# Transposed attention scores of two heads as row tiles, with one exponential over two banks, in a fused attention and mixture-of-experts block

## The reference

```python
Q, K, V = (x @ qw), (x @ kw), (x @ vw)          # 16 heads of 8
Q, K = rope(Q, freq), rope(K, freq)
score = einsum('bhqd,bhkd->bhqk', Q, K) / sqrt(8)
score = score - 1e10 * (1 - causal)
score = score - max(score, axis=-1)
attn = einsum('bhqk,bhkd->bhqd', softmax(score), V)
x = layernorm(x + merged @ ow)
gates = top-2 of softmax(x @ router_w + router_b), renormalised
h = silu(x @ w1[e]) * (x @ w3[e]);  out = sum_e gates[e] * (h @ w2[e])
x = layernorm(x + out)
```

## Time and profile before

| | |
|---|---|
| time, median of 3 runs | 498.72 us (497.11 to 499.74) |
| span of the profiled execution | 495.2 us |
| mean granted TensorE clock | 0.962 |
| projections, rope and pass S of group 0 | 0 to 58 us |
| seven `STEADY` stages | 58 to about 299 us |
| `LAST` | about 299 to 331 us |
| expert phase | 331 to 495 us |

### The profile page before, as it was taken

How to read it: one execution, slowest core, us unless ns; L and a number is a source line. 1 busy time by engine, 2 the same in 40 slices (tenths; PEclk the granted TensorE clock), 3 DMA queues, 4 the chain that set the end, 5 groups by cost and what they waited for, 6 DMA issues and landing times.

```text
span 495.2 us, 10480 instructions
## 1 busy us (share of the span) xinstructions
PE 463.4 (94%) x2676; PEld 296.0 (60%) x2676; DVE 323.8 (65%) x802; ACT 285.1 (58%) x594; POOL 166.9 (34%) x167
## 2 busy tenths in 40 slices
PE   5779999999999999999999999989999999999992
PEld 2346555555554654655655545447887787787781
DVE  3879757777677676777776774313656756756743
ACT  1311146765766766767657666956565565565560
POOL 4524010230411402402304112126645564564661
PEclk9986579999999999999999999999999999999997
DMA  7877411212112112202121000000000000000000
GB/s 249 267 226 192 122 21 26 68 33 66 40 19 64 40 19 64 57 18 67 37 65 39 3 1 3 2 0 1 1 1 3 21 0 0 21 0 0 22 0 22
DMA packets 41738, 23.49 MB, mean 47 GB/s; under 512 B 31280, under 2 KB 33968, under 8 KB 41712
## 3 DMA queue, kind: packets, MB, share of 16 engines
q1 hardware_dynamic: 41712, 23.18, 17.1%
HBM read 14.26 MB, written 8.65 MB: 46 GB/s over the span
## 4 chain that ended last, share of the span: by engine, by line
PE 77%; DVE 7%; issue 4%; ACT 4%; DMA 4%; SPq 3%; POOL 1%; DVEq 0%; ACTq 0%; POOLq 0%
PE bank L960 20%; PE bank L975 15%; PE bank L1044 14%; PE bank L938 14%; PE bank L1055 7%; DVE maxima L703 2%; PE bank L993 2%; DMA k_scratch<-rope_lo 2%; PE bank L941 2%; ACT num L600 1%; DVE num L763 1%; DVE num L836 1%; ACT num L539 1%; SPq L314 1%; PE bank L1020 1%
## 5 line engine op out<-in xcount | busy, mean ns | idle before, releaser
L539 ACT ACTIVATE num<-bank 128x512 f32<-128x512 f32 (+3 forms) x384 | 168.8, 495 | 101.6 <-PE bank L960 99.1
L703 DVE TENSOR_REDUCE maxima<-bank 128x1 f32<-128x512 f32 (+15 forms) x384 | 182.3, 519 | 66.9 <-PE bank L941 46.2
L960 PE MATMUL bank<-q_op,k_op 128*128 128x512 f32 (+3 forms) x384 | 148.2, 419 | 2.8 <-ACT num L539 1.7
L938 PE MATMUL bank<-k_op,q_op 128*128 128x512 f32 (+15 forms) x384 | 126.3, 369 | 3.4 <-issue 2.9
L437 POOL TENSOR_SCALAR_AFFINE_SELECT num<-num 128x512 f32<-128x512 f32 x64 | 40.6, 635 | 226.0 <-ACT num L539 224.1
L960 PEld LDWEIGHTS bank<-q_op,k_op 128*128 128x128 f32 x384 | 71.4, 197 | 69.1 <-ACT num L539 62.0
L468 POOL TENSOR_TENSOR q_op<-num,q_op 128x512 fp32r<-128x512 f32 x64 | 82.4, 1290 | 63.6 <-ACT q_op L593 60.3
L938 PEld LDWEIGHTS bank<-k_op,q_op 128*128 128x128 f32 x384 | 77.0, 202 | 19.2 <-DVE maxima L703 10.9
L1044 PE MATMUL bank<-q_op,w_hi 128*128 (+1 forms) x256 | 81.9, 401 | 1.7 <-DVE num L836 1.6
L975 PE MATMUL bank<-num,v_op 128*32 128x512 f32 (+3 forms) x768 | 82.5, 503 | 0.0
L836 DVE TENSOR_TENSOR num<-bank,num 128x512 f32<-128x512 f32 x64 | 44.2, 691 | 58.5 <-ACT num L600 54.8
(11 more groups left out here) (86 smaller groups left out, 315.7 us busy)
## 6 DMA issues: line engine op xcount, KB each, us to landing
k_op<-k_scratch SPq DMA_DIRECT2D x16, 256.0 KB, 2.7
q_op<-q_scratch SPq DMA_DIRECT2D x64, 52.0 KB
w_raw<-in_w_all SPq DMA_DIRECT2D x6, 512.0 KB, 4.3
q_scratch<-rope_hi SPq DMA_DIRECT2D x8, 256.0 KB, 3.1
k_scratch<-rope_hi SPq DMA_DIRECT2D x8, 256.0 KB, 3.6
xT<-in_x_feat SPq DMA_DIRECT2D x4, 256.0 KB, 6.1
k_scratch<-k_op SPq DMA_DIRECT2D x2, 512.0 KB, 6.2
q_scratch<-rope_lo SPq DMA_DIRECT2D x4, 256.0 KB, 3.9
```

What stands on the lines that cost most here:

```text
L539: act.activation(num[:, t % PB, h, off:CH], t_bank[k % TB][:, off:CH], ACT.Exp, scale=scale)\
L703: dve.tensor_reduce(maxima[:, half, j:j + 1], s_bank[k % SB][:, 0:width], AX.X, ALU.max)\
L938: ins = pe.matmul(s_bank[k % SB][:, 0:width], q_op[u][:, j, :, :].rearrange("p h q -> p (h q)"), k_op[u][:, lo:lo + width], start=True, st ...
L960: pe.matmul(t_bank[k % TB][:, off:CH].rearrange("p (j q) -> p j q", q=QD), k_op[w][:, kt * P:(kt + 1) * P], q_op[w][:, c * NB + off // QD: ...
```

## The change

Pass T now takes two heads in one step. Each of the two matmuls uses only its own head's 32 partitions of `k_op` and `q_op`, as a row tile of the array at row 32 x head, and they write into two neighbouring banks; one ScalarE instruction then takes the exponential over both banks (2 x up to 512 values on each partition). The T steps of a stage become 24. The T side has two pairs of banks, four in all, and the S side keeps two banks. The places of `MROWS`, `NORM` and the `C` steps are renumbered to the new count of T steps, and the interleaving list comes out of the same rule with the new counts.

```diff
+HP = GH // 2
-T_UNITS = [(c, kt, h) for c in range(NC) for kt in range(TI * (c + 1)) for h in range(GH)]
+T_UNITS = [(c, kt, h) for c in range(NC) for kt in range(TI * (c + 1)) for h in range(HP)]
-SB = 3
-TB = 3
+SB = 2
+TB = 2
-C_FROM, C_EVERY = 4, 3
+C_AT = [2 + 3 * r // 2 for r in range(C_STEPS)]
-MROWS_AT, NORM_AT, MROWS0_AT, NORM0_AT = 5, 12, 19, 25
+MROWS_AT, NORM_AT, MROWS0_AT, NORM0_AT = 2, 6, 9, 12
...
-        bank = [ctx.enter_context(nc.psum_tensor(f"bank{i}", [P, CH], F32)) for i in range(8)]
-        s_bank, t_bank, o_bank, small_bank = bank[0:3], bank[3:6], bank[6], bank[7]
+        s_bank = [ctx.enter_context(nc.psum_tensor(f"s_bank{i}", [P, CH], F32)) for i in range(SB)]
+        t_bank = [ctx.enter_context(nc.psum_tensor(f"t_bank{i}", [P, 2, CH], F32)) for i in range(TB)]
...
-                        act.activation(num[:, t % PB, h, off:CH], t_bank[k % TB][:, off:CH], ACT.Exp, scale=scale)\
+                        act.activation(num[:, t % PB, 2 * h:2 * h + 2, off:CH], t_bank[k % TB][:, :, off:CH], ACT.Exp, scale=scale)\
                             .then_inc(t_exped, 1)
...
-                        pe.matmul(t_bank[k % TB][:, off:CH].rearrange("p (j q) -> p j q", q=QD),
-                                  k_op[w][:, kt * P:(kt + 1) * P],
-                                  q_op[w][:, c * NB + off // QD:(c + 1) * NB, h, :], start=True, stop=True)\
-                            .then_inc(t_ready, 1)
+                        for i in range(2):
+                            head = 2 * h + i
+                            rows = slice(head * QD, (head + 1) * QD)
+                            ins = pe.matmul(t_bank[k % TB][:, i, off:CH].rearrange("p (j q) -> p j q", q=QD),
+                                            k_op[w][rows, kt * P:(kt + 1) * P],
+                                            q_op[w][rows, c * NB + off // QD:(c + 1) * NB, head, :],
+                                            start=True, stop=True, tile_position=(head * QD, 0))
+                        ins.then_inc(t_ready, 1)
```

More of the change, by code:

```diff
@@ L45 @@
 SEG_T = [sum(u[0] == c for u in T_UNITS) for c in range(NC)]
-NPV = NT // GH
-SB = 3
-TB = 3
+NPV = NT // HP
+SB = 2
+TB = 2
 HB = 4
@@ L60 @@
 S_LATE, S_EARLY = 0, 3
-MROWS_AT, NORM_AT, MROWS0_AT, NORM0_AT = 5, 12, 19, 25
+MROWS_AT, NORM_AT, MROWS0_AT, NORM0_AT = 2, 6, 9, 12
 def stage_plan(with_s, with_t):
     s_units = S_UNITS if with_s else []
-    t_units = [(u, 0) for u in T_UNITS[GH:]] if with_t else []
-    t_units += [(u, 1) for u in T_UNITS[:GH]] if with_s else []
+    t_units = [(u, 0) for u in T_UNITS[HP:]] if with_t else []
+    t_units += [(u, 1) for u in T_UNITS[:HP]] if with_s else []
     def s_work(units):
@@ L94, in stage_plan @@
         plan.append(("T", c, kt, h, ahead))
-        if not with_s and at >= C_FROM and (at - C_FROM) % C_EVERY == 0 and (at - C_FROM) // C_EVERY < C_STEPS:
-            plan.append(("C", (at - C_FROM) // C_EVERY))
+        if not with_s and at in C_AT:
+            plan.append(("C", C_AT.index(at)))
         part = min(1, t_work(t_units[S_LATE:x + 1]) / max(1, t_work(t_units[S_LATE:len(t_units) - S_EARLY])))
@@ L100, in stage_plan @@
             done_s += 1
-        if h == GH - 1 and with_t and not with_s:
-            t = at // GH - 2
+        if h == HP - 1 and with_t and not with_s:
+            t = at // HP - 2
             if t >= 0:
@@ L107, in stage_plan @@
                 plan.append(("OCOPY", 0))
-        elif h == GH - 1 and with_t:
+        elif h == HP - 1 and with_t:
             if kt >= 1:
@@ L168, in sem @@
             return ctx.enter_context(nc.semaphore(name))
-        bank = [ctx.enter_context(nc.psum_tensor(f"bank{i}", [P, CH], F32)) for i in range(8)]
-        s_bank, t_bank, o_bank, small_bank = bank[0:3], bank[3:6], bank[6], bank[7]
+        s_bank = [ctx.enter_context(nc.psum_tensor(f"s_bank{i}", [P, CH], F32)) for i in range(SB)]
+        t_bank = [ctx.enter_context(nc.psum_tensor(f"t_bank{i}", [P, 2, CH], F32)) for i in range(TB)]
+        o_bank, small_bank = (ctx.enter_context(nc.psum_tensor(n, [P, CH], F32)) for n in ("o_bank", "small_bank"))
+        bank = [*s_bank, *(t[:, i, :] for t in t_bank for i in range(2)), o_bank, small_bank]
         q_dram = nc.dram_tensor("q_scratch", (B * H, QROWS, S), F32).ap()
@@ L369, in stage @@
                     if step == ("T", 1, TI, 0, 0):
-                        sp.wait_ge(t_ready, NT * n + SEG_T[0] + TI * GH)
+                        sp.wait_ge(t_ready, NT * n + SEG_T[0] + TI * HP)
                         load_k(s + 1, v, 0)
@@ L429, in stage @@
                     _, c, kt, h, ahead = step
-                    if kt >= TI * c and h == GH - 1:
+                    if kt >= TI * c and h == HP - 1:
                         k = NT * ahead + T_UNITS.index((c, kt, h))
@@ L434, in stage @@
                         pool.sem_inc(pool_turn, 1)
-                        tile = num[:, (k // GH) % PB, :, off:off + P]
+                        tile = num[:, (k // HP) % PB, :, off:off + P]
                         pool.affine_select(out=tile, in_=tile, compare_op=ALU.is_ge, fill=0.0, base=0,
@@ L439, in stage @@
                             .then_inc(masked, 1)
-                    if split and step == ("T", 0, 0, GH - 1, 1):
+                    if split and step == ("T", 0, 0, HP - 1, 1):
                         pool.wait_ge(w_hi_done, n + 1)
@@ L534, in stage @@
                         off = P * max(0, kt - TI * c)
-                        t = k // GH
+                        t = k // HP
                         act.wait_ge(t_ready, NT * n + k + 1)
@@ L970, in stage @@
                             pe.wait_ge(o_copied, 1 + NC * n + c)
-                        pe.wait_ge(t_exped, TB + NT * n + GH * (t + 1))
+                        pe.wait_ge(t_exped, TB + NT * n + HP * (t + 1))
                         if kt >= TI * c:
```

## The result

The changed kernel takes 704.43 us (median of four runs, 699.6 to 708.1) beside 498.69 us for the kernel before: a ratio of 1.414, 95% interval 1.405 to 1.423. The direction was forecast, the size was not: 560 us, and 595 at the upper end of the range.

The account below looks back on a forecast made before the run. TensorE's own order of work was taken as the bound, VectorE close behind. On 495.2 us, seven stages added 61, `LAST` removed 3.5, the prologue added 4.5: 557.2, forecast 560 with 3.5 around the span; 8-in-10 range 512 to 595.

Parts of the forecast that it names:

- Removed streaming: T steps of a steady stage: paired row tiles stream side by side, so 24 T matmuls vanish, 4.5 us less.
- Changes of tiling: Steady stage: 32 new tiling changes between T and other steps, 0.22 us each less loads already exposed, add 6.2 us.
- The rival of free changes: Row tiles neither empty the array nor expose loads, two banks still cost: about 519 us, chance 0.22.
- The second load: T pairs in a steady stage: a second exposed weight load, 0 to 2.6 us, taken as 1.3.
- Waits for two S banks: S steps in a steady stage wait for one of two banks: 7.1 us, 1.4 there today, so 5.7 added.
- the walk: Slot-by-slot pricing of a steady stage's twelve slots: 7.1 us of S bank waits, 42.9 us a stage against 34.3.
- The rival that the bank isn't missed: VectorE's slack keeps S banks free, bank waits add zero, changes are free: about 470 us, chance 0.08.
- Prologue: Back-to-back maxima before the steady stages: two banks slow 13 pairs by 0.35 us each, adding 4.5 us (0 to 8).
- `LAST`: Final attention stage without S steps, paced by ScalarE: paired exponentials save 3.5 us over eight blocks (0 to 5).
- The clock: TensorE: 1.00 in steady stages; rival had 1.2 GHz for about 10 us a stage, 590 us, 0.20 shared with worse emptying.
- worse emptying: Tiling changes: row tiles empty the array worse than column tiles, up to twice 6.2 us; 0.20 shared with half clock.
- a sign of being wrong: Second pair matmul starting 0.2 us or more after the first, S waits under 3 us a stage, or missing change gaps.

Follow-up runs that it names:

- the twin: The changed kernel with T matmuls over the whole array (no row tiles) and every S matmul issued three times: 648.40 us, 1.305 times the kernel before.
- the twins: Two kernels issuing every S matmul three times: the changed kernel with row tiles, 689.3 and 701.7 us, and the same without row tiles, 648.40 us.

## Why the prediction was wrong, point by point

**Removed streaming** (-4.5 us a stage): the mechanism is right. Row tiles of a pair stream side by side: at 410.59 both are recorded within 0.50 us, where the twin's two need 0.74. No run has the saving by itself.

**Changes of tiling** (+6.2): the price of each is right. 0.11 us of emptying and 0.11 of an exposed load, worked out from PV's column tiles, is what row tiles cost at full clock. The rival of free changes is refuted by the twins (they would have been 4 us a stage apart in favour of row tiles).

**The second load** (+1.3): wrong, it is zero; the loads go side by side. Removed, changes and loads sum to +1.7 without it; the twins show +1.2 (to 2.8), an estimate.

**Waits for two S banks** (+5.7): right within 1 or 2 us. The kernel with pairs over the whole array has 41.5 us a stage, 6.8 more than before. The stage shown has 7.7 us of waits for an S bank, where the walk had 7.1. The 1.4 us a stage that I took off was too much: it spread the 10.9 us of the whole span, and in the stages of the kernel before the same row has only this, 0.9 a stage:

```profile
PEld bank L938 <- DVE maxima L703: 6.4, 22, 0.4
```

With the row tiles' +1.2 the stage would be 42.7 us near full clock (an estimate); the walk through the slots had given 42.9. That they agree so closely is in part luck: the second load was put 1.3 too high and the waits about 1 too low. The rival that the bank isn't missed is refuted by +4.2 us a stage with nothing else changed.

**Prologue** (+4.5): undersized, it is +12.2, and +10.9 with two banks alone. The price of a round at the lower clock was right: the loads that wait for a maximum stand at 50.68, 52.26, 53.84 and 55.42, 1.58 us apart, where I had said about 1.6. These rows are of the changed kernel.

```profile
50.68 0.50 PEld L941 LDWEIGHTS s_bank<-k_op,q_op 128*128 128x128 f32 x2 [0.73 <-DVE maxima L706]
52.26 0.52 PEld L941 LDWEIGHTS s_bank<-k_op,q_op 128*128 128x128 f32 x2 [0.70 <-DVE maxima L706]
```

I multiplied by an average of 0.35 us a pair, where 1.58 - 1.00 = 0.58 stood for 13 pairs (7.5 us). The other 4.7 us were not traced further. I had left out the S steps that stand between projections, and the part before the stages ran at a mean clock of 0.73 where the kernel before had 0.82.

**`LAST`** (-3.5): wrong, +5.3. In the kernel with pairs in `LAST` alone the gain is there (-2.4). In the pairs kernel over the whole array `LAST` takes 32.1 us (360.5 to the first expert load at 392.6), with renumbered `C` steps, longer exponentials and a clock of 0.95. Which of these costs its 2 us over the kernel before was not tried; the rest, up to 35.3, goes with the row tiles and a clock of 0.76.

**The clock** is the step that failed. The sum took every stage at full clock ("clock 1.00 in steady stages"). The lower clock stood only as a rival, which shared a chance of 0.20 with worse emptying, at a price of +30 us, for "about 10 us of each stage". The trace has 0.53 over all seven stages. The sum at full clock comes to 41.5 + 1.2 = 42.7 us a stage; measured are 62.4. The remaining 19.7 us a stage, 138 us in all, go with the clock; this is what is left over, not a measurement by itself. I had priced a stretch that TensorE would leave again within each stage. It did leave it, but for about 24 of the 437 us (an estimate from the mean of 0.53). I also looked for the cause in the waits for VectorE, as in the prologue; two banks alone leave the stages at 0.99, and row tiles alone, with somewhat less of these waits (31.4 us instead of 36.1), put them at 0.50. Nothing that I had named as a sign of being wrong would have told: the second matmul of a pair starts within 0.01 us of the first, the waits for S banks are 6.1 us a stage, and the gaps at changes are there.

**What the clock followed** is shown in part. That row tiles take it down is shown twice, by two pairs of kernels that differ in nothing else: 0.98 against 0.50 with three S banks, 0.98 against 0.53 with two. It falls with tiles of 64 rows as well (0.57); it rises with fewer changes of tiling (0.53 to 0.65 over the stages) and with more S matmuls (0.72 with two, 0.91 with three). Both would fit a clock that follows how much TensorE streams between its gaps. But the pairs over the whole array leave TensorE idle for a tenth of a stage and stay at 1.00, so a gap by a wait does not do what a row tile does. Whether it is the emptying at the changes or the smaller tiles is open; column tiles over all rows in T, which would help to tell, were not tried.

## What to carry to other kernels

Row tiles save one stream and cost an emptying and an exposed load at each change of tiling: 0.14 us saved on a pair of 512 columns, 0.10 given back on the step behind it and 0.08 more on the way in where the step ahead uses the whole array, before any clock is counted. Group all tiles of a kind, or leave the array whole where the contraction can be filled with zeros at no cost. And where a change takes matmul streaming away from an engine that is the bound, price the whole phase at the lower clock too, not a part of it: the same steps took 62.4 us instead of an estimated 42.7. With two banks, two steps take at least a full round of a bank (1.58 us in the prologue at 1.2 GHz; 1.28 at 2.4 GHz is an estimate from the rows before), although the reader, VectorE, had 9 us of slack in a stage.

## What the runs showed of the hardware

- Work added can cost nothing: 384 more matmuls gave 677 to 704 us, where the kernel without them takes 704.
- TensorE can be busy by its records in 508.6 of 509.9 us and have a clock of 0.50, and have records in only 36.9 of 41.1 us and a clock of 1.00. The first kernel has row tiles among full-array steps, the second has none.
- The clock has no steady value in such a kernel. Stages of the same loop had 0.81, 0.97 and 0.84 one behind the other, and a stage's time followed, 64.5, 55.9 and 62.9 us.
- Four row tiles of 32 in four banks, issued two by two, passed in 0.51 us at 256 columns, loads and the emptying behind them included. A change of tiling around row tiles cost what it costs around PV's column tiles, about 0.11 us of emptying and 0.11 of an exposed load.
